# Where VectorE and ScalarE split the Toeplitz table of the next pair, in a one-core sequence kernel

## What is computed

```python
# layer 0: a state-space convolution over the 1024 samples of each (sequence, head)
dtA = (-exp(log_A_real) + 1j * A_imag) * exp(log_dt)[:, None]
K = 2 * einsum('hn,hnl->hl', Cs, exp(dtA[:, :, None] * arange(1024))).real
y = causal_convolution(x * mask, K) + x * mask * D[:, None]     # mask: sample < length
x = x + y * mask
# layer 1: a dense projection with two of eight low-rank experts
base = einsum('btd,od->bto', x, W)
top2 of (x @ Wr.T + 5.0 * onehot(language)), softmax of the two -> gates
x = x + base + 2.0 * einsum('bter,bte,eor->bto', einsum('btd,erd->bter', x, A), gates, B)
```

## Time and profile before

| | |
|---|---|
| median of 3 runs | 715.37 us (712.67, 715.37, 715.88) |
| profiled execution: own time | 714.37 us |
| profiled execution: span | 712.6 us |
| TensorE matmul / weight load busy | 648.1 us (91%) / 617.4 us (87%) |
| VectorE, ScalarE, GpSimd busy | 495.3 us (70%), 464.9 us (65%), 19.1 us (3%) |
| mean granted clock of TensorE | 0.975 of full speed |
| DMA over the span | 43.40 MB, 61 GB/s |

### The profile page before, as it was taken

One profiled execution on the slowest core, in us unless ns is written; L12 is line 12 of the kernel. 1 busy time (PEld: TensorE's weight loads), 2 busy tenths in 40 slices (PEclk: granted clock), 3 DMA queues, 4 the chain that ended last, 5 costly groups with the idle time before them and its releaser, 6 DMA issues.

```text
span 712.6 us, 12371 instructions
## 1 busy us (share of the span) xinstructions
PE 648.1 (91%) x3629; PEld 617.4 (87%) x3629; DVE 495.3 (70%) x1518; ACT 464.9 (65%) x980; POOL 19.1 (3%) x38
## 2 busy tenths in 40 slices
PE   3679778999999999999999999999999999999997
PEld 2478668899898989999898989989898989989997
DVE  8885665776776777766777768676777777676641
ACT  5875666767576767757577766757677776754431
POOL 0000000000000000000000000000000000000000
PEclk9699988999999999999999999999999999999999
DMA  6521122111223222123222221122232211222112
GB/s 184 165 60 31 37 67 68 33 54 47 66 66 66 66 66 41 46 45 66 66 66 66 66 52 47 34 66 66 66 66 66 61 29 57 52 66 38 39 29 60
DMA packets 23904, 43.40 MB, mean 61 GB/s; under 512 B 9896, under 2 KB 14544, under 8 KB 23888
## 3 DMA queue, kind: packets, MB, share of 16 engines
q1 hardware_dynamic: 18608, 26.42, 16.1%
q10 hardware_dynamic: 5280, 16.78, 9.5%
HBM read 26.35 MB, written 16.85 MB: 61 GB/s over the span
## 4 chain that ended last, share of the span: by engine, by line
DVE 34%; PE 22%; issue 21%; ACT 21%; DVEq 1%; ACTq 1%; DMA 0%; SPq 0%
PE pc L1159 13%; DVE state L885 11%; ACT swapped L479 9%; PE pmg L1220 7%; DVE xt L926 5%; ACT s_hi L501 3%; DVE u_lo L837 3%; ACT state L487 3%; ACT L668 2%; DVE t_lo L842 2%; DVE zo_lo L848 2%; DVE gate L959 1%; DVE held L918 1%; DVE k_col L857 1%; DVE c_lo L858 1%
## 5 line engine op out<-in xcount | busy, mean ns | idle before, releaser
L1220 PE MATMUL pmg<-w_hi,y_hi 128*128 128x388 f32 (+1 forms) x768 | 267.4, 348 | 3.1 <-DVE w_lo L828 3.1
L1220 PE MATMUL pmg<-w_lo,y_hi 128*128 128x388 f32 (+1 forms) x768 | 261.7, 341 | 0.0
L1220 PE MATMUL pmg<-w_hi,y_lo 128*128 128x388 f32 (+1 forms) x768 | 261.6, 341 | 0.0
L1220 PEld LDWEIGHTS pmg<-w_hi,y_hi 128*128 128x128 f32 x768 | 145.9, 190 | 4.1 <-DVE w_lo L828 3.6
L1220 PEld LDWEIGHTS pmg<-w_hi,y_lo 128*128 128x128 f32 x768 | 145.9, 190 | 0.4
L1220 PEld LDWEIGHTS pmg<-w_lo,y_hi 128*128 128x128 f32 x768 | 145.6, 190 | 0.0
L479 ACT ACTIVATE swapped<-state 64x128 f32<-64x128 f32 x192 | 59.3, 309 | 87.3 <-DVE state L885 86.0
L524 ACT ACTIVATE result<-pmg 128x388 f32<-128x388 f32 (+1 forms) x96 | 43.2, 452 | 71.8 <-PE pmg L1207 71.3
L885 DVE SCALAR_TENSOR_TENSOR state<-swapped,scan_tab,state 128x192 f32<-128x192 f32 (+1 forms) x240 | 73.8, 349 | 17.1 <-ACT swapped L479 12.7
L918 DVE COPY held<-lang_f 128x1 f32<-128x1 f32 x96 | 14.8, 154 | 78.5 <-PE pc L1159 76.3
L914 DVE TENSOR_TENSOR s_lo<-state,s_hi 128x896 fp32r<-128x896 f32 x32 | 35.0, 1092 | 35.5 <-ACT s_hi L501 35.5
(11 more groups left out here) (206 smaller groups left out, 1068.6 us busy)
## 6 DMA issues: line engine op xcount, KB each, us to landing
rows<-in_x SPq DMA_DIRECT2D x64, 256.0 KB, 5.4
out<-result ACTq DMA_DIRECT2D x62, 256.0 KB, 3.8
toe<-kpad SPq DMA_DIRECT2D x30, 128.0 KB, 5.2
rows<-in_L_cond_W SPq DMA_DIRECT2D x3, 512.0 KB, 6.5
result<-in_L_cond_W SPq DMA_DIRECT2D x3, 512.0 KB, 6.0
w_rows<-in_L_cond_W SPq DMA_DIRECT2D x2, 512.0 KB, 4.4
result<-in_L_cond_A SPq DMA_DIRECT2D x1, 512.0 KB, 5.7
b_rows<-in_L_cond_B SPq DMA_DIRECT2D x2, 256.0 KB, 6.7
```

Source lines behind the costliest of these rows:

```text
L1220: ins = nc.tensor.matmul(pm[:, n, 0:o1 - o0], y[s][:, c, :], w[:, c, o0:o1], start=(c == 0 and y is y_hi and w is w_hi), stop=(c == CH - 1 ...
```

## The change

In the steps of the loop and behind it, ScalarE's and VectorE's `split_toe(b, m + 1)` go to the head of the step, in front of `split_ctr(b, m + 2)`. TensorE's and SyncE's programs, and the first four pairs, stay as they are.

```diff
--- before.py
+++ after.py
@@ -637,6 +637,7 @@
             split_states(0, 3)
 
             def step(b, m, rows_left=True, kernels=True):
+                split_toe(b, m + 1)
                 if rows_left:
                     split_ctr(b, m + 2)
                     split_obs(b, m + 2)
@@ -644,7 +645,6 @@
                 if rows_left:
                     split_rows(b, m + 2)
                 ratios(b, m)
-                split_toe(b, m + 1)
                 if kernels and m == 0:
                     act.wait_ge(gen_staged, b + 1)
                     turns_of(None, True)
```

## The result

The changed kernel takes 692.63 us (median of 4 runs, 690.85 to 693.01), the one before beside it 714.71 us. The ratio is 0.9689, its 95% interval 0.966 to 0.972. The forecast was 714.4 us with a range from 710.8 to 719.5.

What follows compares the result with a forecast made beforehand. The prediction took TensorE, busy 91% of the span, to wait for t_lo because VectorE is full before the convolution. Terms of +0.1 and -1.1 gave -1.0 us on a 712.6 us span, so 714.4 us, range 710.8 to 719.5.

Steps and rivals of the forecast that it cites:

- The step that failed: VectorE's queue before the convolution: t_lo is late because VectorE is full, and the convolution needs u_lo and t_lo alike.
- Sum: 0.00 us a step: VectorE: t_lo's move delays u_lo by 0.35 us, to when t_lo ended before, so the last operand comes no earlier.
- The prediction's own sign of being wrong: TensorE at the convolution: the forecast is wrong if its summed waits move by more than 3 us either way.
- The bound on the gain: TensorE's waits for t_lo from 100 to 700 us: at most 23.2 us, 3% of the time, could be given back.
- The term of t_lo and t_hi in their queues: VectorE's queue moves by 0.35 us, ScalarE's by 0.36; taken as 0.01 us in 14 steps, 0.1 us in all.
- gated 0.35 us later with m = 1: TensorE's turn of the gates moves to 342.36, covered by the convolution's own wait until 343.58; idle time only changes place.
- TensorE's start behind its last operand: Weight loads after the last operand: 0.18 us taken, 1.1 us gained; bounds from 4.1 us gained (0.07) to 5.9 lost.
- the slower rival: TensorE passing met waits behind u_lo: 0.11 us each, price 5.9 us, giving 721.3 us; chance 0.08.
- The toe table: SyncE's load, issued 0.35 us later and wanted at the next step's head: cover 10.7 us, was 13.7, so no wait.
- the rows: SyncE's load behind the table's, moved 0.35 us later: the rows have most of a step, so no wait.
- the first and last step: Steps (1, 0) and (15, 0): no gain, since TensorE isn't waiting for t_lo there; the sum runs over 27 steps.
- a faster one with 0.16: TensorE starts at once behind u_lo, 0.07 us after its end: price 4.1 us, giving 711.3 us; chance 0.16.

Runs made afterwards that it cites:

- Run 1: The kernel before, with only VectorE's t_lo of pair i+1 moved in front of u_lo of pair i+2, behind the router: 691.39 us.
- run 5: The kernel before, with u_lo of pair i+2 made in two halves and t_lo between them: 699.82 us.
- run 6: The changed kernel, with the convolution of pair i+1 waiting for u_lo of pair i+2, which it doesn't read: 711.18 us.
- run 4: The changed kernel, with VectorE's powers behind the router instead of in front of it, in steps with m = 1: 686.74 us.
- Run 2: The kernel before, with only t_hi moved to the head of ScalarE's step; t_lo stays behind u_lo: 720.85 us.
- run 3: The kernel before, with four more already met waits between tlo and merged in TensorE's convolve: 716.86 us.

## Why the prediction was wrong

**The step that failed** stands in the first part: "the convolution needs u_lo and t_lo alike: they stand next to each other". It does need a u_lo, but its own pair's. The description of the kernel ahead of the prediction has it right (u_lo of i+2, t_lo of i+1, convolve(i+1)), and the wait in TensorE's program is `ulo_ready, i + 1`, which the last step's u_lo has met. The name of the tile, which has no pair in it in a row of the trace, was read in place of the count in the semaphore. From this came "Sum: 0.00 us a step. The last operand of the convolution is now u_lo in place of t_lo, at the same time." What the runs showed in its place: t_lo leaves the stretch behind gated, 1.56 us from the start of u_lo to the end of t_lo, and the convolution may start as soon as the gates are turned. Run 1 has the gain by leaving u_lo behind t_lo, run 5 has two thirds of it for half of u_lo, and run 6 loses 18.5 us of it when the convolution is made to wait for the foreign u_lo. The prediction's own sign of being wrong, TensorE's waits at the convolution moving by more than 3 us, came true with 23.2 us.

- **The bound on the gain was too low.** The 23.2 us of the earlier trace rows are the idle time in front of the matmuls, and the prediction called them "all that a better order of VectorE's work could give back". This change gave back 22.1 us of span. But run 4, which is also no more than an order of VectorE's work, stands 28 us under the kernel before (40.54 - 38.39 = 2.15 us a pair, and 715.2 against 686.74 us). The weight loads of the same line had more idle time, and 0.16 us for gated stood in front of it with m = 1:

```profile
  issue: 29.2, 27
  DVE t_lo L842: 23.2, 27
```

- **The term of t_lo and t_hi in their queues** was right: 0.34 us on each engine, half_sum's wait unchanged, no wait for ScalarE at VectorE's head. Run 2 shows what it costs where only one of the two queues moves.
- **gated 0.35 us later with m = 1** was seen, and its cover named as "the convolution's own wait". That cover went, so the item that had been put at nothing became the kernel's remaining stall, 0.51 us in 13 steps. Run 4 took it away: 686.74 us against 692.63, 5.9 us or 0.45 us in each of the 13 steps (0.41 by the pairs of the profiles).
- **TensorE's start behind its last operand** was no term of this change at all, since the operand isn't last any more. As a size, 0.18 us was wrong and the lower bound of 0.07 right (0.06 to 0.08 in run 6), and the slower rival's 0.11 us per met wait is 0.014 in the steps (run 3).
- **The toe table, the rows, the first and last step** showed no wait from the change, as forecast. The table's cover before the change comes out of the rows as 14.1 us and not 13.7 (319.56 + 20.70 - 320.97 - 5.2); nothing hangs on it.
- **The rivals** had a faster one with 0.16, but by another mechanism, and its 711.3 us bounded what it could give. None of the rivals asked whether the instruction between the old and the new place is one that the waiting engine needs.

## What to carry to other kernels

When an instruction is moved past others on a queue, write down for each of them which iteration's data it makes and from when somebody wants it, by the number in the wait and not by the tile's name. An urgent operand that stands behind work for a later iteration costs that work's whole length, and two neighbours changing places can be worth 3%. After the change, look at the waits that were hidden in front of the one that went: the next stall is there, and here its removal was worth another 0.9%.

## What the runs showed of the hardware

A wait that is already met cost TensorE's queue 0.014 us, over the 108 of run 3 that stand in steps where TensorE waits for t_lo; the granted clock of that run from 300 to 345 us was 1.00 of full speed. At its first convolution four of them cost 0.07 us each, at a granted clock of 0.50 (31.5 to 34 us). That is one case, and whether the clock is the reason isn't shown.

The time from the end of VectorE's instruction to the start of the weight load that waits for it doesn't follow from the number of met waits: it is 0.06 us behind u_lo with three met waits after it (run 6), and 0.22 us behind t_lo with one. Before the change it was 0.21 to 0.23 us in all 27 steps. Why the shorter instruction has the longer gap stays open; no run here was made for it.
